# Group sums placed as two 16-bit parts, the mix a slot later, and a new opening and last pass in a graph network layer

## The chip, the cores and the metric

The kernel runs on one core of one Trainium2 chip. The metric is the device time of one execution in microseconds (us); lower is better. A core has five engines with a queue each: TensorE (PE, matmuls), VectorE (DVE), ScalarE (ACT), GpSimd (POOL) and SyncE (SP, which here only issues transfers). Matmuls write to eight PSUM banks of 128 x 512 f32. The engines wait for each other by semaphores that the kernel sets by hand.

## What is computed

x has 6250 rows of 512; 100000 edges (src, dst, weight) are sorted by dst. The rest is weights. Cut to what matters, without the biases' names:

```python
xn  = layernorm(x)
gnn = segment_sum(weight[:, None] * xn[src], dst) @ Wg + b_g
q, k = elu(xn @ Wq + bq) + 1, elu(xn @ Wk + bk) + 1      # 8 heads of 64
v    = xn @ Wv + bv
kv   = einsum('shd,she->hde', k, v)
z    = 1 / einsum('shd,hd->sh', q, k.sum(0))
mix  = einsum('shd,hde,sh->she', q, kv, z) @ Wp + bp
x1   = x + gnn + mix
xm   = layernorm(x1)
g    = mean over rows of (relu(xm @ G1.T + b) @ G2.T + b2)   # 8 gates
W1m, W2m, b1m, b2m = W + sum_e g[e] * tvW[e], ...           # merged weights
res  = xm + relu(xm @ W1m.T + b1m) @ W2m.T + b2m
out  = x1 + layernorm(res) * lng + lnb
```

## The kernel before

The rows are 49 tiles of 128 (T = 49, the last one short). Every f32 factor of a large product is held as two f16 parts (high and low), and a product is three f16 passes over them: 12 matmuls of 128x512 for a tile and a weight of 512 x 512. The accumulator `acc` holds all rows of x in SBUF.

*Opening and head.* SP loads Wg, Wk and Wq into `stage`, the biases, x and the edges; DVE takes the weights' maxima, POOL spreads them over the partitions, DVE makes the scales, ACT the high parts of the weights and DVE the low parts. Then 49 row ticks: layernorm (ACT `normalise`, DVE `low_parts`), stores of the f16 parts of x to `x_rows` and, transposed on PE, to `xt_rows`, and y = xn @ Wg, stored to `y_rows`. The work of each engine for one tick is written in its own `head_tick`.

*The middle.* It runs in slots s. The edges are cut into 196 groups of 512 (NGR), one for each slot; in a slot POOL issues four indirect gathers of 128 rows of `y_rows` each, for a ring of three groups. PE's `part(s)` sums each 128 edges of a group into 32 targets with 12 matmuls against 0/1 times weight matrices (`hots`), which gives a bank of 128 partial rows. `keep_part(s)` on ACT copies the bank to `part32` in f32, `place(s)` on PE moves the rows to their place in a tile with a f32 matmul against a 0/1 matrix (`plc`), and `add_group(s)` on DVE adds the bank to the two tiles of `acc` that it may touch. Around these, tiles of the attention part run at fixed slots: K tile t at slot -2 + 11t/6 (`k_product` on PE; `feature` on ACT and `k_whole` on DVE one slot later; `k_higher`, `k_lower`, `k_sum`; `m_product`, k times x, on PE three slots later, with x reloaded from `x_rows` as two f16 parts). From slot 89 (TURN) the K sums are turned and merged into `KVP`. From slot 95 Q tile t runs at slot 95 + 2t: `q_product`, `feature` one slot later, DVE's `q_shares` (kf, qk, den, rden, qs), `q_higher` and `q_lower` two slots later, `turn_q` on PE at three, `mix` (KVP with the turned q) on PE at four and `add_mix` on DVE at five. The order of work on each engine is that of a loop over the slots, written out for each engine:

```python
for s in range(K_FIRST, SLOTS_END):          # PE
    turn_q(tile at s - 3); part(s); mix(tile at s - 4)
    m_product(tile at s - 3); place(s - 1)
    k_product or q_product(tile at s)
for s in range(K_FIRST, SLOTS_END):          # DVE
    add_group(s - 2); add_mix(tile at s - 5)
    k_sum, k_lower, q_lower(tile at s - 2)
    place_pair or hot_pair; k_whole or q_shares(tile at s - 1)
```

*Tail, gate and last pass.* The tail normalises `acc` and makes the gate's hidden layer. The gate merges the weights; PE waits for all eight `tvW2` blocks and DVE splits b2 in three parts while it does. The last pass runs over the tiles: `hidden` and the second product on PE, residual `res`, bn_stats, bn_aggr, `nbr` and the gain `zr` on DVE, `zr` = res scaled and shifted on ACT, and on POOL two additions, `acc` + lnbb and `ob` = `zr` + `acc`; SP stores `ob`.

## Time and profile before

| | us |
|---|---|
| median of 3 runs | 1880.41 |
| lowest, highest | 1877.25, 1880.98 |
| the profiled execution | 1881.32 |
| its span, first to last instruction | 1879.5 |
| opening; head | 0 to 41.5; to 238 |
| start of the middle; K part | to 262; to 797 |
| turn to Q; Q part | to 845; to 1445 |
| tail; gate | to 1634; to 1676 |
| last pass | to 1879.5 |

A row of a timeline has a start, a duration, the engine, the line of the kernel and the operation, what it writes and reads, how many instructions are merged in it (x12), and in brackets how long the engine stood idle before it and what ended the wait. "issue" is idle time for which the profile shows nothing; "remote" a releaser that it doesn't know. In a table by stretches each engine has its busy time with the number of its instructions; PEclk is the granted clock of PE as a share of the full one.

### The profile page before, as it was taken

The numbers are of one execution on the slowest core, as the hardware profiler recorded it, in microseconds if no ns is written. First come the engines' busy times: TensorE is split into PE (matmuls) and PEld (weight loads), VectorE is DVE, ScalarE is ACT, GpSimd is POOL, SyncE is SP. The second block draws the span as 40 slices with busy tenths as digits, with TensorE's granted clock in tenths as the row PEclk, the third lists the DMA queues.
The fourth block names the chain that finished last, engine by engine and source line by source line (L and its number), as shares of the span: only waits on it lengthen the run. The fifth ranks groups of instructions, "written<-read, shape, count | busy, mean of one in ns | idle before, by whom it ended". The sixth has DMA issues, their size and how long they took to land.

```text
span 1879.5 us, 27602 instructions
## 1 busy us (share of the span) xinstructions
PE 1549.2 (82%) x8551; PEld 672.3 (36%) x8551; DVE 1212.1 (64%) x2230; ACT 702.8 (37%) x1098; POOL 919.1 (49%) x919
## 2 busy tenths in 40 slices
PE   0699968888988898787888888888887799888883
PEld 0345423333333333243333333333333444453331
DVE  7888734554544555456776777676667666468996
ACT  3266522222222232212332333333333677425554
POOL 3000056666666666646666666666663000016776
PEclk9799989999999999978999999999999799989996
DMA  5389777777777777746666666666665422333332
GB/s 182 127 297 324 272 238 227 220 214 224 225 227 223 227 225 225 213 123 193 194 197 200 196 195 196 195 196 197 196 197 154 159 78 79 115 115 107 134 134 83
DMA packets 149271, 353.64 MB, mean 188 GB/s; under 512 B 24773, under 2 KB 30551, under 8 KB 149155
## 3 DMA queue, kind: packets, MB, share of 16 engines
q0 software_dynamic: 62720, 205.57, 37.0%
q1 hardware_dynamic: 84926, 145.42, 22.6%
q8 instruction: 60, 0.98, 0.2%
q10 hardware_dynamic: 1509, 1.21, 0.2%
q14 instruction: 56, 0.46, 0.1%
HBM read 287.93 MB, written 65.38 MB: 188 GB/s over the span
## 4 chain that ended last, share of the span: by engine, by line
PE 37%; DVE 18%; another core or an unknown queue 16%; issue 14%; ACT 9%; DMA 2%; DVEq 1%; ACTq 0%; SPq 0%; POOL 0%; POOLq 0%
PE bank L1550 26%; PE bank L1659 4%; PE bank L1633 4%; ACT mb L642 2%; PE bank L1649 2%; DVE acc L1164 2%; ACT part L636 2%; DVE st L1058 1%; PE bank L1592 1%; ACT qT L663 1%; DVE res L1511 1%; DVE zr L1539 1%; DVE zl L1092 1%; ACT zh L598 1%
## 5 line engine op out<-in xcount | busy, mean ns | idle before, releaser
L850 POOL DMA_INDIRECT rows<-y_rows,idxT x784 | 767.9, 979 | 613.3 <-issue 395.1
L1164 DVE SCALAR_TENSOR_TENSOR acc<-bank,maskt,acc 128x512 f32 x392 | 275.4, 744 | 200.3 <-remote 107.4
L642 ACT ACTIVATE mb<-bank,ones,ncols 128x512 f32<-128x512 f32 x98 | 76.6, 782 | 527.5 <-remote 290.6
L1550 PE MATMUL bank<-KVP,qT 128*128 128x512 f16 x588 | 168.2, 446 | 72.1 <-ACT qT L663 62.1
L1649 PE MATMUL bank<-rows,hots 128*32 128x512 f16 x2352 | 194.3, 402 | 38.7 <-issue 35.1
L1659 PE MATMUL bank<-part,plc 128*128 128x512 f32 x392 | 212.1, 622 | 12.3 <-ACT part L636 6.0
L636 ACT COPY part<-bank 128x512 f32<-128x512 f32 x196 | 113.0, 577 | 192.7 <-remote 145.5
L1550 PE MATMUL bank<-Wg,xtb 128*128 128x512 f16 x588 | 143.3, 396 | 25.6 <-DVE xtb L1103 25.5
L1550 PE MATMUL bank<-Wk,xta 128*128 128x512 f16 x588 | 142.9, 394 | 1.2 <-issue 1.0
L1633 PE MATMUL bank<-xr,kh 128*128 128x512 f16 x392 | 124.8, 402 | 16.7 <-DVE kl L1191 13.4
L1649 PEld LDWEIGHTS bank<-rows,hots 128*32 128x32 f16 x2352 | 78.1, 143 | 166.4 <-issue 144.3
L1550 PE MATMUL bank<-Wq,xta 128*128 128x512 f16 x588 | 135.4, 380 | 0.0
L1550 PE MATMUL bank<-ztg,G 128*128 128x512 f16 (+1 forms) x624 | 134.8, 368 | 0.0
L1550 PEld LDWEIGHTS bank<-KVP,qT 128*128 128x128 f16 x588 | 61.0, 111 | 174.5 <-ACT qT L663 81.4
L1205 DVE SCALAR_TENSOR_TENSOR kf<-bank,cols,mb 128x512 f32<-128x512 f32 x49 | 36.8, 750 | 111.8 <-ACT mb L645 86.6
L1184 DVE SCALAR_TENSOR_TENSOR kf<-bank,cols,mb 128x512 f32<-128x512 f32 x49 | 36.6, 746 | 106.9 <-issue 55.7
L874 POOL PARTITION_ALL_REDUCE mxa<-mx x1 | 0.3, 350 | 206.5 <-DVE mx L1462 206.5
L1659 PEld LDWEIGHTS bank<-part,plc 128*128 128x128 f32 x392 | 68.2, 193 | 67.3 <-issue 45.1
L891 POOL TENSOR_TENSOR ob<-zr,acc 128x512 f32<-128x512 f32 x49 | 63.0, 1287 | 55.4 <-DVE zr L1539 53.3
L1550 PEld LDWEIGHTS bank<-Wg,xtb 128*128 128x128 f16 x588 | 56.7, 101 | 92.8 <-DVE xtb L1103 19.7
L1550 PEld LDWEIGHTS bank<-Wk,xta 128*128 128x128 f16 x588 | 55.1, 100 | 76.4 <-issue 22.6
L1550 PE MATMUL bank<-xd,W1m 128*128 128x512 f16 (+1 forms) x312 | 72.6, 387 | 9.9 <-DMA xd<-zt_rows 6.2
(278 smaller groups left out, 2324.0 us busy)
## 6 DMA issues: line engine op xcount, KB each, us to landing
xta<-xt_rows SPq DMA_DIRECT2D x98, 256.0 KB
x_rows<-xhl SPq DMA_DIRECT2D x49, 256.0 KB, 2.6
xt_rows<-xtb SPq DMA_DIRECT2D x49, 256.0 KB, 3.0
y_rows<-yb SPq DMA_DIRECT2D x49, 256.0 KB, 2.5
rows<-y_rows,idxT POOLq DMA_INDIRECT x784
xr<-x_rows SPq DMA_DIRECT2D x49, 256.0 KB
zt_rows<-ztg SPq DMA_DIRECT2D x49, 256.0 KB, 2.0
acc<-in_x SPq DMA_DIRECT2D x48, 256.0 KB, 3.1
```

What stands on the lines that cost most here:

```text
L598: nc.scalar.activation(to, flat(acc, t), ACT.Identity, scale=rs[:, bass.ds(t, 1)], bias=nb[:, bass.ds(t, 1)]).then_inc(loop.high, 1)
L636: nc.scalar.copy(part32[:, s % 2, :], edge_bank(s)[:, :]).then_inc(part_kept, 1)
L642: nc.scalar.activation(mb[:, :], of[:, :], ACT.Relu, scale=ncols[:, col:col + 1], bias=ones[:, 0:1]).then_inc(f_min, 1)
L850: pool.indirect_dma_start(out=rows[:, slot].rearrange("p a d -> p (a d)"), out_offset=None, in_=y_rows, in_offset=bass.IndirectOffsetOnAxi ...
L891: pool.tensor_tensor(ob[:, b, :], zr[:, b, :], flat(acc, t), ALU.add).then_inc(ob_made, 1)
L1164: nc.vector.scalar_tensor_tensor(out=flat(acc, tile + m), in0=placed_bank(s)[:, :], scalar=maskt[:, m, s:s + 1], in1=flat(acc, tile + m), ...
L1184: nc.vector.scalar_tensor_tensor(out=kf[:, b, :], in0=bank[5][:, :], scalar=cols[:, 1:2], in1=mb[:, :], op0=ALU.mult, op1=ALU.max).then_in ...
L1205: nc.vector.scalar_tensor_tensor(out=kf[:, 0, :], in0=q_bank(t)[:, :], scalar=cols[:, 2:3], in1=mb[:, :], op0=ALU.mult, op1=ALU.max).then_ ...
L1550: ins = nc.tensor.matmul(dest, lhs, rhs, start=(n == 0 and only), stop=(n == len(pairs) - 1), skip_group_check=not only)
L1633: ins = nc.tensor.matmul(bank[c][:, :], (kh, kl)[p][:, b, s], xr[:, b, q, :], start=isinstance(t, int) and t == 0 and i == 0, stop=isinsta ...
L1649: ins = nc.tensor.matmul(edge_bank(s)[W * i:W * i + W, :], hots[:, k, p, :, m + i], rows[:, K4 * (s % RING) + i, q, :], start=n == 0, stop ...
L1659: nc.tensor.matmul(placed_bank(s)[:, :], plc[:, s // WG % 3, s % WG, :], part32[:, s % 2, :], start=True, stop=True).then_inc(placed, 1)
```

## The change

Place: `keep_part` becomes `part_higher`, which writes the bank times 2^-14 as f16; a new `part_lower` on DVE makes the rest, bank times 2^-14 less the high part, from the same bank; `place` is two f16 matmuls that add up. `plc` is f16 and written in another layout. The factors of the weights and of the mask are changed to fit. `mix` and `add_mix` run one slot later.

Opening: only Wg is loaded first, on ACT's queue; the x tiles come ahead of the edges, the biases last. Wk and Wq are loaded at tick 40 of the head (KQ_AT), the edges are packed in memory at tick 41, their maxima are taken at ticks 42 and 43, the scales at 44, the high parts at 45 and 46, the low parts at 47 and 48. Both bias splits and their copies are POOL's, after the scales. x isn't stored as parts; in the K part raw x is loaded again, ACT's `x_again` makes both x and its f16 part, and DVE's `x_lower` the rest. Wp is loaded after the K part, gfc1 at Q tile 3, and the maximum and the scale of gfc1 are taken at slots TURN + 18 and TURN + 28.

Gate and last pass: `tvW2` comes in pairs and PE adds pair by pair; the split of b2 stands after the merged W1. In the last pass the mean comes from the sum that `res` yields beside its output, the variance from a Square on ACT with a sum; DVE makes `cen` and `ob`, POOL keeps only `acc` + lnbb, and the result is stored five tiles later instead of four.

```diff
@@ constants
-SLOTS_END = max(NGR + 2, Q_FIRST + Q_SPACE * (T - 1) + 6)
+SLOTS_END = max(NGR + 2, Q_FIRST + Q_SPACE * (T - 1) + 7)
+PART, WEIGHT = float(2.0 ** -14), float(2.0 ** -8)
+OUT_LAG = 5
+TV2_PAIRS = ((6, 7), (0, 1), (2, 3), (4, 5))
+KQ_AT = (T // U - 1) * U
@@ SP, head_stores
-                if exists(g, j):
-                    t = tile_at(g, j)
-                    sp.wait_ge(head.low, t + 1)
-                    sp.dma_start(row_tile(x_rows, t), xhl[:, j % 4].rearrange("p a d -> p (a d)")
-                                 ).then_inc(x_kept[j % 4], 16)
+                if isinstance(g, int) and tile_at(g, j) == KQ_AT:
+                    sp.wait_ge(tabled, 3)
+                    for k, (dest, w) in enumerate(((Wkraw, Wk), (Wqraw, Wq))):
+                        sp.dma_start(dest[:, :, :], w.rearrange("(c p) n -> p c n", p=P)).then_inc(w_loaded[k + 1], 16)
+                if isinstance(g, int) and tile_at(g, j) == KQ_AT + 1:
+                    pack_edges()
@@ SP, load_rows
-                at_least(sp, m_done, t - 1)
-                sp.dma_start(xr[:, b].rearrange("p a d -> p (a d)"), row_tile(x_rows, t)).then_inc(xr_in[b], 16)
+                at_least(sp, xr_high, 2 * (t - 1))
+                    sp.dma_start(xraw[:, b], row_tile(x[0:(T - 1) * P, :], t)).then_inc(xr_in[b], 16)
@@ ACT
-                nc.scalar.copy(part32[:, s % 2, :], edge_bank(s)[:, :]).then_inc(part_kept, 1)
+                nc.scalar.activation(phl[:, s % 2, 0, :], edge_bank(s)[:, :], ACT.Copy, scale=PART).then_inc(part_high, 1)
+            def x_again(t):
+                b = t % 2
+                act.wait_ge(xr_in[b], 16 * (t // 2) + 16)
+                at_least(act, xr_low, t - 1)
+                at_least(act, m_done, t - 1)
+                for to in (xn32[:, b, :], xr[:, b, 0, :]):
+                    nc.scalar.activation(to, xraw[:, b, :], ACT.Identity, scale=rs[:, t:t + 1], bias=nb[:, t:t + 1]
+                                         ).then_inc(xr_high, 1)
@@ DVE, the middle
+            def part_lower(s):
+                dve.wait_ge(part_high, s + 1)
+                at_least(dve, placed, s - 1)
+                nc.vector.scalar_tensor_tensor(out=phl[:, s % 2, 1, :], in0=edge_bank(s)[:, :], scalar=PART,
+                                               in1=phl[:, s % 2, 0, :], op0=ALU.mult, op1=ALU.subtract).then_inc(part_low, 1)
+            def x_lower(t):
+                b = t % 2
+                dve.wait_ge(xr_high, 2 * t + 2)
+                at_least(dve, m_done, t - 1)
+                nc.vector.tensor_tensor(xr[:, b, 1, :], xn32[:, b, :], xr[:, b, 0, :], ALU.subtract).then_inc(xr_low, 1)
                 add_group(s - 2, tile)
+                part_lower(s - 1)
+                if s == TURN + 18:
+                    gate_largest()
+                if s == TURN + 28:
+                    gate_scale()
-                t = tile_of(q_slot, s - 5)
+                t = tile_of(q_slot, s - 6)
@@ PE, the middle
-                pe.wait_ge(part_kept, s + 1)
+                pe.wait_ge(part_low, s + 1)
-                nc.tensor.matmul(placed_bank(s)[:, :], plc[:, s // WG % 3, s % WG, :], part32[:, s % 2, :],
-                                 start=True, stop=True).then_inc(placed, 1)
+                accumulate(placed_bank(s)[:, :], [(plc[:, s // WG % 3, :, s % WG], phl[:, s % 2, h, :]) for h in range(2)]
+                           ).then_inc(placed, 1)
-                t = tile_of(q_slot, s - 4)
+                t = tile_of(q_slot, s - 5)
@@ ACT, the last pass
+                    nc.scalar.activation(squares[:, :], res[:, j1, :], ACT.Square, bias=negm[:, par, i:i + 1],
+                                         accum_out=dev2[:, par, i:i + 1]).then_inc(squared, 1)
-                    nc.scalar.activation(zr[:, b, :], res[:, j4, :], ACT.Identity, scale=rsr[:, j4 // Q4, j4 % Q4:j4 % Q4 + 1],
-                                         bias=nbr[:, j4 // Q4, j4 % Q4:j4 % Q4 + 1]).then_inc(zr_made, 1)
@@ POOL, the last pass
-                    pool.tensor_tensor(ob[:, b, :], zr[:, b, :], flat(acc, t), ALU.add).then_inc(ob_made, 1)
@@ DVE, the last pass
-                    nc.vector.bn_stats(st6[:, j % Q4, :], res[:, j, :]).then_inc(six_made, 1)
-                    nc.vector.tensor_tensor(zr[:, b, :], zr[:, b, :], lngb[:, :], ALU.mult).then_inc(gained, 1)
+                    nc.vector.scalar_tensor_tensor(out=cen[:, :], in0=res[:, j5, :], scalar=negm[:, par5, i5:i5 + 1],
+                                                   in1=lngb[:, :], op0=ALU.add, op1=ALU.mult).then_inc(gained, 1)
+                    nc.vector.scalar_tensor_tensor(out=ob[:, b5, :], in0=cen[:, :], scalar=rsr[:, par5, i5:i5 + 1],
+                                                   in1=flat(acc, t5), op0=ALU.mult, op1=ALU.add).then_inc(ob_made, 1)
```

Three places show how instructions move. First PE in the Q part, one tile (two slots), from the turning of a q on: `hots` with `rows` is a part, `plc` a place, `KVP` the mix, `Wq` the next product. Before:

```order
L1691 MATMUL bank<-ident_51,qhl 128x128 x8
L1649 MATMUL bank<-rows,hots 32x512 x12
L1659 MATMUL bank<-part_146,plc 128x512
L1649 MATMUL bank<-rows,hots 32x512 x12
L1550 MATMUL bank<-KVP_113,qT 128x512 x12
L1659 MATMUL bank<-part_146,plc 128x512
L1550 MATMUL bank<-qrows,ones_54 128x512
L1550 MATMUL bank<-Wq_104,xta 128x512 x12
```

After:

```order
L1772 MATMUL bank<-ident_51,qhl 128x128 x8
L1730 MATMUL bank<-rows,hots 32x512 x12
L1631 MATMUL bank<-KVP_116,qT 128x512 x12
L1631 MATMUL bank<-phl,plc 128x512 x2
L1730 MATMUL bank<-rows,hots 32x512 x12
L1631 MATMUL bank<-phl,plc 128x512 x2
L1631 MATMUL bank<-qrows,ones_54 128x512
L1631 MATMUL bank<-Wq_107,xta 128x512 x12
```

The mix has moved from between the second part and its place to between the first part and its place, and each place is two matmuls.

Second DVE in the Q part, from the last step of the shares to the end of the same slot. `acc<-bank,maskt,acc` twice is `add_group`, `phl` the new low part, `acc<-bank,cols,acc` is `add_mix`. Before:

```order
L1225 TENSOR_TENSOR qs<-qk,rden 128x512
L1295 TENSOR_LOAD tileof
L1295 ISA x2
L1164 ISA
L1164 SCALAR_TENSOR_TENSOR acc<-bank,maskt,acc 128x512
L1164 ISA
L1164 SCALAR_TENSOR_TENSOR acc<-bank,maskt,acc 128x512
L1232 SCALAR_TENSOR_TENSOR qhl<-qs,qhl 128x512
L1138 TENSOR_TENSOR plc<-iota_100,tgt 128x128x2
```

After:

```order
L1297 TENSOR_TENSOR qs<-qk,rden 128x512
L1377 TENSOR_LOAD tileof
L1377 ISA x2
L1221 ISA
L1221 SCALAR_TENSOR_TENSOR acc<-bank,maskt,acc 128x512
L1221 ISA
L1221 SCALAR_TENSOR_TENSOR acc<-bank,maskt,acc 128x512
L1231 SCALAR_TENSOR_TENSOR phl<-bank,phl 128x512
L1240 SCALAR_TENSOR_TENSOR acc<-bank,cols,acc 128x512
L1304 SCALAR_TENSOR_TENSOR qhl<-qs,qhl 128x512
L1195 TENSOR_TENSOR plc<-iota_103,tgt 128x256
```

The low part stands behind the shares and the group's adds; `add_mix` has come from the other slot of the tile.

Third DVE in the last pass, one tile. Before:

```order
L1511 SCALAR_TENSOR_TENSOR res<-bank,cols,zq 128x512
L1516 BN_STATS st_59<-res 128x6
L1520 RECIPROCAL rsr<-sd_60 128x4
L1522 SCALAR_TENSOR_TENSOR nbr<-var_58,rsr 128x4
L1539 TENSOR_TENSOR zr<-zr,lngb 128x512
```

After:

```order
L1594 SCALAR_TENSOR_TENSOR res,rsum<-bank,cols,zq 128x512
L1605 SCALAR_TENSOR_TENSOR cen<-res,negm,lngb 128x512
L1609 TENSOR_SCALAR negm<-rsum 128x1
L1612 REGISTER_ALU
L1617 ISA
L1617 SCALAR_TENSOR_TENSOR ob<-cen,rsr,acc 128x512
```

Statistics and gain are gone, `cen` and `ob` stand behind the residual of a later tile.

## Rows read from the trace of the kernel before

**Rows 1.** The page: the span, and its groups of instructions for mix and Wq product.
```profile
span 1879.5 us, 27602 instructions
...
L1550 PE MATMUL bank<-KVP,qT 128*128 128x512 f16 x588 | 168.2, 446 | 72.1 <-ACT qT L663 62.1
...
L1550 PE MATMUL bank<-Wq,xta 128*128 128x512 f16 x588 | 135.4, 380 | 0.0
```

**Rows 2.** Table by stretches: length, busy us of each engine, clock, DMA share, GB/s.
```profile
41.50:238.00 196.50, 165.95 (x1009) 85.54 (x1009) 157.91 (x316) 104.57 (x157) 0.86 (x2) 0.93 0.70 249
262.00:797.00 535.00, 468.00 (x2475) 180.91 (x2473) 275.38 (x501) 149.36 (x235) 346.37 (x359) 0.96 0.73 222
845.00:1445.00 600.00, 518.29 (x2994) 217.64 (x2994) 416.12 (x741) 192.97 (x296) 388.51 (x392) 0.94 0.67 195
1676.00:1879.50 203.50, 154.69 (x631) 58.31 (x631) 165.35 (x248) 110.31 (x161) 132.13 (x98) 0.89 0.32 113
```

**Rows 3.** Timeline of one tile, Q part: start, duration, engine, line, [idle before <-releaser].
```profile
952.10 0.95 POOL L850 DMA_INDIRECT rows<-y_rows,idxT  x1 [0.30 <-issue]
...
953.01 2.76 PE L1550 MATMUL bank<-Wq,xta 128*128 128x512 f16 x12
...
955.81 0.78 ACT L642 ACTIVATE mb<-bank,ones,ncols 128x512 f32<-128x512 f32 x1 [5.72 <-issue]
...
957.29 0.75 DVE L1205 SCALAR_TENSOR_TENSOR kf<-bank,cols,mb 128x512 f32<-128x512 f32 x1 [1.12 <-issue]
...
958.01 0.88 PE L1649 MATMUL bank<-rows,hots 128*32 128x512 f16 x12
...
959.81 1.46 POOL L850 DMA_INDIRECT rows<-y_rows,idxT  x1 [1.78 <-PE bank L1649]
...
960.66 1.41 DVE L1164 SCALAR_TENSOR_TENSOR acc<-bank,maskt,acc 128x512 f32 x2 [0.21 <-issue]
...
961.13 4.37 PE L1550 MATMUL bank<-KVP,qT 128*128 128x512 f16 x12 [2.25 <-ACT qT L663]
...
965.30 1.14 PE L1659 MATMUL bank<-part,plc 128*128 128x512 f32 x2
...
966.69 2.76 PE L1550 MATMUL bank<-Wq,xta 128*128 128x512 f16 x12
```

**Rows 4.** Timeline, Q part, a mix after a shorter wait.
```profile
1216.27 2.76 PE L1550 MATMUL bank<-KVP,qT 128*128 128x512 f16 x12 [0.51 <-ACT qT L663]
```

**Rows 5.** Timeline of the K part at 499 us.
```profile
499.93 2.76 PE L1550 MATMUL bank<-Wk,xta 128*128 128x512 f16 x12
...
503.43 0.60 PE L1633 MATMUL bank<-xr,kh 128*128 128x512 f16 x2
...
503.87 0.38 PE L1633 MATMUL bank<-xr,kl 128*128 128x512 f16 x1
...
506.87 0.78 ACT L642 ACTIVATE mb<-bank,ones,ncols 128x512 f32<-128x512 f32 x1 [5.98 <-remote]
```

**Rows 6.** Timeline of the opening and of the start of K.
```profile
14.65 10.65 SPq L432 DMA_DIRECT2D srow<-in_dst  x1
...
41.51 0.80 PE L1592 MATMUL bank<-ident,xhl 128*128 128x128 f16 x6 [41.51 <-DVE xhl L1092]
...
248.28 0.58 PE L1550 MATMUL bank<-krows,ones 3*128 3x512 bf16 x1 [11.76 <-DMA xta<-xt_rows]
```

**Rows 7.** Groups with shapes kept apart: the weights' maxima, the gain in the last pass.
```profile
L1539 DVE TENSOR_TENSOR zr<-zr,lngb 128x512 f32<-128x512 f32 x49 | 63.2, 1289 | 15.1 <-ACT zr L774 14.6
...
L938 DVE TENSOR_REDUCE mx<-stage 128x1 f32<-128x2048 f32 x3 | 6.9, 2285 | 7.5 <-DMA stage<-in_L_gnn_weight 3.4 <-DMA stage<-in_L_mix_Wk 2.2 <-DMA stage<-in_L_mix_Wq 2.0
```

**Rows 8.** Timeline of the last pass: its first and last residual, a gain behind it.
```profile
1682.05 0.75 DVE L1511 SCALAR_TENSOR_TENSOR res<-bank,cols,zq 128x512 f32<-128x512 f32 x1 [3.90 <-PE bank L1550]
...
1858.87 0.74 DVE L1511 SCALAR_TENSOR_TENSOR res<-bank,cols,zq 128x512 f32<-128x512 f32 x1
...
1867.19 0.69 DVE L1539 TENSOR_TENSOR zr<-zr,lngb 128x512 f32<-128x512 f32 x1 [0.40 <-ACT zr L774]
```

371 lines of the change are left out of this document (210 added, 161 removed).

## The prediction

> **What bounds the kernel now.** I read the head of the page, then the table by stretches, then short timelines inside the two long stretches, since those show which wait ends last. The profiled execution's span is 1879.5 us [rows 1] and its own time 1881.32, so 1.8 us lie around the span; the median of the three runs, 1880.41, is 0.9 below that execution. The stretches [rows 2] are the opening to 41.5, the head (49 row tiles) to 238, the K part of the middle 262 to 797, the Q part 845 to 1445 and the last pass from 1676. K and Q hold 1135 of the 1880 us. In K 89 groups of edges pass in 535 us, 6.0 us each; in Q 49 tiles pass at two groups each, 12.1 us a tile. PE is the busiest engine in both (468.0 of 535, 518.3 of 600), but it isn't full, and POOL needs less than the time that passes too: a gather is issued every 0.95 + 0.30 = 1.25 us [rows 3], a group has four of them, so POOL could start a group every 5.0 us, 10.0 a Q tile.
>
> The loop that ends last in Q reads off one tile [rows 3]: the product of x and Wq starts at 953.01; ACT's feature starts 2.80 later, when the product ends; DVE's first step at 957.29; its last step of the shares is over before the adds of the even group at 960.66 (1.41 us). Beside it PE waited 2.25 us for the turned q and then ran the mix in 4.37 us. Another mix, after a wait of 0.51 us, took 2.76 [rows 4]. Over all 49 tiles such idle is 62.1 us, 1.3 a tile, and a matmul of the mix takes 446 ns in the mean where one of the Wq product takes 380 [rows 1]: 12 × 0.066 = 0.8 us a tile, so about half of the mixes run slow. The place at 965.30 and the next product at 966.69 stand behind the mix. 1.3 + 0.8 is the 2 us a tile between POOL's 10.0 and 12.1.
>
> In K one fact limits what a timeline proves: the product is recorded from 499.93 for 2.76 us, yet the feature starts at 506.87 and the trace names no releaser [rows 5]. There PE's recorded ends are early, or something outside the records holds. I keep wide bounds for it.
>
> **The change, part by part.**
>
> *Place in two 16-bit matmuls.* Before, a place is two f32 passes; from the place at 965.30 to the next product with its bias rows between are 1.39 us [rows 3], some 0.95 of them the place. Two f16 matmuls of the same 128x512 occupy 503.87 − 503.43 = 0.44 us [rows 5]. PE saves 0.51 us a group, 1.0 in two groups. ACT's copy from the bank becomes a scaled one (a tenth of a us more, ACT is idle two thirds of the time) and is free. DVE gains an operation per group, with the bank and one other operand, 0.75 us as kf at 957.29 [rows 3], and has a shorter comparison for places, which now writes 16 bits; that is under +1.5 on some 8.5 us of DVE work a Q tile, beside 12.1 us: DVE isn't the bound by its sum.
>
> But it is on the path now. The low part of group s−1 stands behind the adds of group s−2, and in the Q part these stand behind the feature and the shares. The loop becomes: product 2.80, feature to the first DVE step 1.48, shares to the start of the adds 3.37, adds 1.41, low part 0.75, then place and bias rows 1.39 less 0.51, and the next product: **10.7 us a tile**, by rows of the clear case [rows 3]. From the product's end to the place are 7.0 us. PE has for them: turning q, a part and a place (2.2 us to 958.01, now 0.5 less), a part of 0.88 and a mix at full clock of 2.7, in all 5.3. It will stand 1.7 us before that place.
>
> *Mix one slot later.* The turned q is then ready a slot ahead, and the 2.25 us wait at 961.13 goes [rows 3]. What is late next is just this place: the idle moves from before the mix to before the place. The question is PE's clock. The mix took 4.37 after 2.25 us of idle and 2.76 after 0.51 [rows 3, 4]; 1.7 lies nearer the first. If the product behind the place then runs at the lower level of 1.2 GHz, the loop is 10.7 + 1.6 = 12.3. The Trainium skill ("TensorE: Matmul & The Clock Gate", section "HAM oscillation — how this bites in real kernels") says that a kernel whose PE keeps pausing falls to the lower clock again and again; by that the Q part would stay at 12.3 a tile. The mix at 4.37 agrees, the mix at 2.76 shows that a short pause does nothing. I take the middle, 11.5, since about half of the mixes now run slow after a wait: 49 × −0.6 = **−29 us** (ends: −69 and +10).
>
> *K part.* The same place saving, 0.51 of PE a group; added are two ACT passes over 512 columns that remake x (0.78 each, as the feature's at 955.81 [rows 3]) and one DVE subtraction (0.7, under kf's 0.75) a K tile, against a reload of the same 256 KB. ACT is busy 149 of 535 us, DVE 275 [rows 2], so they hide; if the subtraction came to stand ahead of the low part, a tile would lose up to its 0.7. The lower bound is POOL's 10.0 for two groups where 12.0 pass: 44.5 × −2.0 = −88; the upper is 0, since the place also gets its new wait there and the DMA engines are already busy 0.73 of the time [rows 2]; at 10.0 they would be at 0.88, above the 0.70 and 0.73 of the busiest stretches there. I take half: **−44**.
>
> *Opening.* Only Wg is loaded ahead of the first tile. The first transposes start at 41.51 [rows 6]. Two maxima of 2.29 us [rows 7], their waits for weights, half of the scale chain, the low part of Wk (2048 columns like a maximum, about 2.3) and the split of a bias on DVE leave the stretch before it. Two ways bound it: SP stays blocked for 10.65 us on the small row of edges at 14.65 [rows 6], which no longer stands ahead of the first four x loads but still ahead of the next (−16), or it doesn't block (−26). I take **−19**. What is moved comes back in ticks 42 to 48 of the head, where DVE is busy 158 of 196.5 us and PE 166 [rows 2]: 2 × 2.3 for maxima, 2 × 2.3 for low parts and 14 small operations of 0.2 = 12.0, plus 0.9 for the edge scales, **+13**; SP issues the two loads and seven small ones in ticks 40 and 41, ahead of that tick's stores: **+3** (0 to +8). The stores of x_rows go, 12.8 MB where the DMA engines are busy 0.70 of the time [rows 2]: **−3** (−6 to 0). At the start of K the first product waited 11.76 us for its data [rows 6] behind weights of which one load is now elsewhere: **−3** (−6 to 0). POOL now splits both biases after tick 44; it ends just before K starts, by the old split's pace, 0 to +4. Head together **−9** (−22 to +4).
>
> *Gate.* Loads by pairs let PE work as data comes; the b2 split leaves slack and stands on DVE's path with five operations of at most 0.69 each, 3.4 us. Net **+1.5** (−2 to +4). The gate maximum (2.29) leaves the start of the tail: **−1**. It now stands in the Q part, once.
>
> *Last pass.* 48 tiles from 1682.05 to the last residual at 1858.87 [rows 8], 3.68 us each. On DVE a tile had residual, statistics, gain 1.29 mean, hidden's low part; POOL two adds. Now DVE has residual 0.74, centring 0.75, a small negation 0.15, result 0.75, hidden's part 0.4: 2.8, with two operations of two SBUF inputs beside one POOL add. The gain is 0.69 when alone and 1.29 in the mean [rows 7, 8], so 0.6 is lost to POOL a tile; with one POOL add left I keep 0.6: 3.4. That is 48 × −0.28 = **−13**. The Trainium skill ("SBUF — State Buffer", section "Who interferes with whom") calls the port pair of DVE and GpSimd an exclusive lock; the rows at 0.69 against a mean of 1289 ns agree. If both new operations paid 0.6, a tile would take 4.0 and the pass would lose 15 instead. The end, 20.6 us from that residual to the span's end, holds a ping-pong of ACT, DVE and POOL for five tiles; without POOL's add in each: **−4**. Together −17 (−30 to +11).
>
> **The sum:** −9 − 44 − 29 − 1 + 1.5 − 17 = −98.5. 1881.3 − 98.5 = 1782.8; less 0.9 to the median: **1782**.
>
> **The rivals.**
> A. *The forecast*, about 1782; own range 1735 to 1820. For it: PE's idle before the mix goes by the order alone, and the place is half as long. 0.50.
> B. *The middle keeps its pace.* 6.0 and 12.1 stay, because gathers and their landing (or what the trace doesn't name at 506.87) set them. For it: unnamed releasers, DMA at 0.73 and 0.67. Against: POOL's own pause before a group is ended by a part on PE, 1.78 us at 959.81 [rows 3]. Only the ends gain, −9 − 1 + 1.5 − 17 = −25.5: 1855. 0.25.
> C. *The floors are reached*: 10.0 in K, 10.7 in Q, full clock. −25.5 − 88 − 69: 1698. Against: nothing in the trace runs long at POOL's own pace. 0.12.
> D. *Slower.* The place waits behind DVE's chain and PE's clock falls each time: place, bias rows and product at the lower level put 1.6 + 0.9 us on the loop, 13.2 a Q tile (49 × 1.1 = +54), and in K 0.2 for two groups (+9); with the ends −25.5 that is +37.5: 1918. It decides from the point at which the pause before the place costs as much clock as the mix's did and reaches the place itself. For it: 4.37 against 2.76. Against: PE's pause would be shorter than the mix's. 0.09.
> E. *It doesn't do what it says:* the wait for the turned q stays, or the loads in ticks 40 to 48 disturb the head by more than the opening gains; all terms cancel, 1880. 0.04.
>
> **How the numbers follow.** The likeliest is A, 1782. The range reaches to B's 1855 with a few us for the last pass's bound, and down to 1700, which leaves out most of C and D: 1700 to 1860. A run of this kernel can be told from no change at about 0.2% (3.8 us). Faster: A, B, C and half of what is left of E, 0.89; slower 0.09; same 0.02.
>
> **What would show it.** In Q: period between Wq products, 11.5 (B 12.1, C 10.7, D 13.2); PE's largest wait is that of the place for phl from DVE, 1.5 to 2 us, and none for qT is left; products of 4.4 us after it mean the lower clock. In K: 11.0 for two groups, POOL's waits shorter. Opening: first transposes at about 22. Head: ticks 42 to 48 stretched by some 13 us. Last pass: residuals 3.4 apart, cen or ob near 1.4 in the mean of one of them. I am wrong if the period in Q doesn't change though the mix waits no more, or if the DVE operation isn't what the place waits for.

## The result and the profile after

The changed kernel took 1926.67 us in the median of four runs (1920.8 to 1933.14), the kernel before 1880.0 beside it: a ratio of 1.0251, 95% interval 1.0216 to 1.0287. It is 47 us slower. Forecast was 98 faster, in a range of 1700 to 1860. What came is near the rival called slower (D, 1918). Its mechanism is there in part: the place waits behind VectorE's chain, and PE's clock falls behind it in some tiles. That the sum is so near is luck, as the table below shows: D had +54 in Q, +9 in K and −25.5 at the ends, and +14.5, +25.5 and about 0 came, with 2.6 more in the turn and 9.3 behind the last product. The profiled execution has a span of 1931.3 us, 51.8 more than before [rows 1]; it is the longest of the four, 6.5 us over their median.

The page after, the groups that answer to [rows 1] and the place:

```profile
span 1931.3 us, 28100 instructions
...
L1631 PE MATMUL bank<-phl,plc 128*128 128x512 f16 x392 | 129.2, 414 | 224.5 <-DVE phl L1231 161.0
...
L1631 PE MATMUL bank<-Wq,xta 128*128 128x512 f16 x588 | 180.0, 470 | 0.0
...
L1631 PE MATMUL bank<-KVP,qT 128*128 128x512 f16 x588 | 137.6, 383 | 3.4 <-issue 3.4
```

A matmul of the Wq product takes 470 ns where it took 380, one of the mix 383 where it took 446, and PE stands idle for 224.5 us before places, 161 of them ended by VectorE's low part `phl`. The table by stretches, as in [rows 2]:

```profile
41.50:238.00 196.50, 156.60 (x949) 79.97 (x947) 152.28 (x303) 98.80 (x146) 20.88 (x24) 0.92 0.58 193
262.00:797.00 535.00, 422.83 (x2365) 159.46 (x2364) 336.42 (x620) 204.08 (x317) 342.78 (x345) 0.91 0.70 214
845.00:1445.00 600.00, 470.79 (x2869) 190.11 (x2868) 441.95 (x822) 187.94 (x283) 376.26 (x382) 0.89 0.64 189
1676.00:1931.00 255.00, 195.22 (x894) 88.43 (x891) 177.61 (x349) 119.63 (x228) 73.13 (x51) 0.87 0.33 113
```

The granted clock falls from 0.96 to 0.91 in K and from 0.94 to 0.89 in Q; no engine is busier than 0.79 of Q. One tile of the Q part, the engines of [rows 3]:

```profile
960.88 0.68 DVE L1231 SCALAR_TENSOR_TENSOR phl<-bank,phl 128x512 f16<-128x512 f32 x1
...
961.61 0.61 PE L1631 MATMUL bank<-phl,plc 128*128 128x512 f16 x2 [2.89 <-DVE phl L1231]
...
962.15 0.39 PE L1631 MATMUL bank<-qrows,ones 3*128 3x512 bf16 x1
...
962.47 4.45 PE L1631 MATMUL bank<-Wq,xta 128*128 128x512 f16 x12
...
966.96 0.78 ACT L669 ACTIVATE mb<-bank,ones,ncols 128x512 f32<-128x512 f32 x1 [6.47 <-PE bank L1631]
```

PE waits 2.89 us for the low part, the place follows, and the product behind it takes 4.45 us instead of 2.76. In K and Q 36 of 98 such products take 4 us or more; before it was 4.

Where the 51.8 us are, by the times at which work of the same kind starts (first transposes, first part, last Wk product, first and last Wq product, last mix, first copy of a turned tile in the tail, last gate activation, first and last residual of the last pass, end of span):

| stretch | before | after | difference | forecast |
|---|---|---|---|---|
| opening | 41.5 | 21.2 | −20.3 | −19 |
| head to first part | 221.1 | 235.1 | +14.1 | +10 |
| K part | 511.8 | 537.3 | +25.5 | −44 |
| turn | 65.2 | 67.8 | +2.6 | 0 |
| Q part | 587.8 | 602.3 | +14.5 | −29 |
| last product to last mix | 13.7 | 23.0 | +9.3 | 0 |
| tail | 193.7 | 195.4 | +1.6 | −1 |
| gate to first residual | 47.2 | 51.5 | +4.2 | +1.5 |
| last pass | 176.8 | 180.9 | +4.0 | −13 |
| end | 20.6 | 17.0 | −3.7 | −4 |

### The profile page after: what moved, and what is told of

The parts are those of the page before. It is cut to its first block and busy times, and to the rows that moved or that the text cites. A ratio compares the mean times of both kernels' runs of the same rounds, so it can differ in the third digit from the quotient of the medians.

```text
span 1931.3 us, 28100 instructions
## 1 busy us (share of the span) xinstructions
PE 1506.3 (78%) x8551; PEld 645.9 (33%) x8551; DVE 1305.7 (68%) x2516; ACT 771.6 (40%) x1244; POOL 877.6 (45%) x884
## 3 DMA queue, kind: packets, MB, share of 16 engines
q1 hardware_dynamic: 78623, 132.68, 20.5%
## 5 line engine op out<-in xcount | busy, mean ns | idle before, releaser
L1631 PE MATMUL bank<-phl,plc 128*128 128x512 f16 x392 | 129.2, 414 | 224.5 <-DVE phl L1231 161.0
L1631 PE MATMUL bank<-Wq,xta 128*128 128x512 f16 x588 | 180.0, 470 | 0.0
L663 ACT ACTIVATE phl<-bank 128x512 f16<-128x512 f32 x196 | 114.8, 586 | 156.9 <-remote 86.9
L1730 PE MATMUL bank<-rows,hots 128*32 128x512 f16 x2352 | 176.0, 405 | 0.3 <-issue 0.3
L1631 PE MATMUL bank<-Wk,xta 128*128 128x512 f16 x588 | 164.1, 438 | 0.0
L1631 PE MATMUL bank<-KVP,qT 128*128 128x512 f16 x588 | 137.6, 383 | 3.4 <-issue 3.4
L1231 DVE SCALAR_TENSOR_TENSOR phl<-bank,phl 128x512 f16<-128x512 f32 x196 | 133.0, 679 | 0.0
L1631 PEld LDWEIGHTS bank<-phl,plc 128*128 128x128 f16 x392 | 31.2, 101 | 295.8 <-DVE phl L1231 189.5
L932 POOL TENSOR_TENSOR acc<-acc,lnbb 128x512 f32 (+1 forms) x49 | 72.4, 1478 | 117.7 <-ACT zq L794 117.7
L1631 PEld LDWEIGHTS bank<-Wq,xta 128*128 128x128 f16 x588 | 63.9, 116 | 102.5 <-issue 68.2
```

The source lines that it names most:

```text
L663: nc.scalar.activation(phl[:, s % 2, 0, :], edge_bank(s)[:, :], ACT.Copy, scale=PART).then_inc(part_high, 1)
L932: pool.tensor_tensor(flat(acc, t), flat(acc, t), lnbb[:, :], ALU.add).then_inc(based, 1)
L1231: nc.vector.scalar_tensor_tensor(out=phl[:, s % 2, 1, :], in0=edge_bank(s)[:, :], scalar=PART, in1=phl[:, s % 2, 0, :], op0=ALU.mult, op1= ...
L1631: ins = nc.tensor.matmul(dest, lhs, rhs, start=(n == 0 and only), stop=(n == len(pairs) - 1), skip_group_check=not only)
L1730: ins = nc.tensor.matmul(edge_bank(s)[W * i:W * i + W, :], hots[:, k, p, :, m + i], rows[:, K4 * (s % RING) + i, q, :], start=n == 0, stop ...
```

## Experiments

The kernels ran on four chips: beside e1 to e4 the kernel before took 1882 us, beside e6 to e9, on another, 1868, beside all others, on two more, 1728 to 1730. I call the last two clean. Nearly all of the difference lies in the middle: on the clean chip K takes 443.7 us instead of 511.8, the turn 51.0 instead of 65.2 and Q 509.7 instead of 587.8, while opening, head, last pass and end agree to 2 us, tail and gate together to 3, and from the last product to the last mix it takes 4 longer. So ratios are to the kernel before on the same chip, run beside it.

Each stretch below is read from one profiled execution, and these differ by some us where nothing was changed: e2 alters nothing in K, and its K is 507.2 beside 511.8. Single differences under about 5 us in a stretch prove nothing. The edits are shown shortened to their point.

### One part alone, one part undone (chip of 1882)

e1, place alone in the kernel before:

```diff
-    nc.scalar.copy(part32[:, s % 2, :], edge_bank(s)[:, :])
+    nc.scalar.activation(phl[:, s % 2, 0, :], edge_bank(s)[:, :], ACT.Copy, scale=PART)
     add_group(s - 2, tile)
+    part_lower(s - 1)
-    matmul(placed_bank(s), plc, part32)
+    accumulate(placed_bank(s), [(plc, phl high), (plc, phl low)])
```

> The kernel before with one part of the change alone: the place in two 16-bit matmuls, its low part made by VectorE behind the adds; the mix stays at slot + 4 and opening and last pass stay. Theory 1 (the place now waits for VectorE's low part, which stands behind the feature, the shares and the adds, and PE's clock falls behind that wait): the K part gets slower by some 20 us and the Q part by 10 to 40, since both the mix and the place now end a wait there: 1910 to 1940. Theory 2 (the middle lost time by the x that is made again in the K part and by the work that was moved into it, not by the place): the place saves PE 0.5 us a group, so 1840 to 1880.

Measured: 1884.66, ratio 1.0015 (0.998 to 1.0049). K 517.3 (+5.5), Q 581.0 (−6.8). Neither theory: no gain of 0.5 us a group, and no loss beyond the noise as long as the mix stands where it stood.

e2, mix alone:

```diff
-                t = tile_of(q_slot, s - 4)
+                t = tile_of(q_slot, s - 5)
                 if t is not None:
                     mix(t)
```

> The kernel before with the mix and its addition one slot later, nothing else. Theory 1 (PE's idle before the mix and its slow mixes cost 2 us a Q tile): the wait for the turned q goes, the Q part falls from 588 us to 540 to 570, and the end of the middle grows by one slot: 1840 to 1875. Rival (gathers or another loop set 12 us a Q tile, and the idle only moves): the Q part stays within 5 us of 588 and the total is 1880 to 1890.

Measured: 1866.95, ratio 0.9927 (0.9899 to 0.9955). The wait for the turned q is gone (3.5 us of idle in place of 72.1 [rows 1]) and a mix matmul takes 389 ns instead of 446, 2 us a tile:

```profile
L1550 PE MATMUL bank<-KVP,qT 128*128 128x512 f16 x588 | 141.4, 389 | 3.5 <-issue 3.3
```

But Q (572.7) gains only 15.1 us, 0.3 a tile, and the end of the middle gives 6.8 back. The total lies in the range of theory 1, but not the Q part, which was to fall to 540 to 570. The 2 us were not what stood between GpSimd's 10.0 and the 12.1.

e3, the changed kernel with the place of before:

```diff
-                part_lower(s - 1)
-                accumulate(placed_bank(s), [(plc, phl high), (plc, phl low)])
+                matmul(placed_bank(s), plc, phl in f32)
```

> The changed kernel with the place of before: f32 copy by ScalarE, f32 matmul, no low part on VectorE; all the rest as changed. Theory 1 (place): from first part to last K product 510 to 518 us instead of 538, Q part under 588, total 1850 to 1880. Theory 2 (the x made again costs the K part its 26 us): that stretch stays at 535 to 540, total 1900 to 1925.

Measured: 1891.85, ratio 1.0046 (1.0021 to 1.0071) where the changed kernel had 1.0251, so some 38 us less. K 519.7, Q 578.4. The total lies between the two theories. Beside the rest of the change the place costs 18 of K's 25.5 us and 24 in Q; 8 us of K are left, little over the noise, of which x made again is the likeliest cause. Alone the place cost 5.5 in K and nothing in Q (e1). So in K place and x made again cost more together than apart, and in Q the place costs only beside something else, most likely the mix's new slot; neither pair was run by itself.

e4, the low part earlier, and in the last pass the hidden layer's low part earlier:

```diff
                 add_group(s - 2, tile)
-                part_lower(s - 1)
...
+                part_lower(s)
                 for slot_of, after, work in ((k_slot, 1, k_whole), (q_slot, 1, q_shares)):
@@ last pass, DVE
                 res of tile t
+                hidden_low(...)
                 cen, negm, ob
-                hidden_low(...)
```

> The changed kernel with two orders on VectorE changed. The low part of group s is made at the end of slot s, ahead of the feature's and the shares' work, instead of behind the adds of slot s + 1. In the last pass the low part of the hidden layer stands right behind the residual, ahead of centring and result. Theory 1 (what costs is where the low part stands): PE's wait for it all but goes, the K part falls under 512 us and the Q part to 540 to 575. Theory 2: both keep 538 and 602. In the last pass, if the lock between VectorE's operations and GpSimd's addition hit the hidden layer's low part (1598 ns in place of 804) and this operation holds PE, a tile falls from 3.77 to 3.3 to 3.5 us, 13 to 20 us in all; if PE or ScalarE sets the pace, it stays at 3.7. Total by theory 1: 1810 to 1860; by theory 2 with the lock gone: 1905 to 1915.

Measured: 1885.83, ratio 1.0022 (0.9995 to 1.0049) where the changed kernel had 1.0251: some 43 us of the 47 are back, 20.5 of them by the last pass (160.4 instead of 180.9, 3.34 us a tile) and 23 in Q (579.1). The idle before places that VectorE's low part ends falls from 161 us to 11. But K stays at 532.0, and Q and the total are above what theory 1 had for them: for the middle it came only in part.

The last pass is settled by two views. The changed kernel, three groups of VectorE and a tile:

```profile
L1582 DVE SCALAR_TENSOR_TENSOR hT<-h,sc,hT 128x512 f16<-128x512 f32 x24 | 38.4, 1598 | 2.3 <-ACT hT L786 2.3
L1605 DVE SCALAR_TENSOR_TENSOR cen<-res,negm,lngb 128x512 f32<-128x512 f32 x49 | 38.2, 780 | 0.1
L1617 DVE SCALAR_TENSOR_TENSOR ob<-cen,rsr,acc 128x512 f32<-128x512 f32 x49 | 36.8, 751 | 9.5 <-DVE cen L1605 8.0
...
1803.02 1.44 POOL L932 TENSOR_TENSOR acc<-acc,lnbb 128x512 f32 x1 [2.54 <-ACT zq L794]
1803.26 1.75 DVE L1582 SCALAR_TENSOR_TENSOR hT<-h,sc,hT 128x512 f16<-128x512 f32 x1
...
1805.14 0.38 PE L1631 MATMUL bank<-krows,qrows 3*128 3x512 bf16 x1 [2.56 <-DVE hT L1582]
```

The same groups in e4:

```profile
L1620 DVE SCALAR_TENSOR_TENSOR ob<-cen,rsr,acc 128x512 f32<-128x512 f32 x49 | 55.3, 1128 | 9.5 <-DVE cen L1608 8.0
...
L1608 DVE SCALAR_TENSOR_TENSOR cen<-res,negm,lngb 128x512 f32<-128x512 f32 x49 | 39.6, 808 | 0.1
...
L1582 DVE SCALAR_TENSOR_TENSOR hT<-h,sc,hT 128x512 f16<-128x512 f32 x24 | 23.9, 995 | 2.3 <-ACT hT L786 2.3
```

GpSimd's addition starts after 2.54 us of idle, when the residual has let ScalarE make the next input; then VectorE is at the hidden layer's low part, which takes 1.75 instead of 0.75, and PE waits 2.56 us for it. In e4 the same overlap falls on `ob` (1128 instead of 751), for which no engine waits.

### The clean chip (1728)

> The kernel before, unchanged, so that its trace and that of the changed kernel come from one chip. The time of the kernel before was 1882 us beside e1 to e4 and 1728 beside e5 and p1 to p3; the middle alone makes the difference. If the chip is one where gathers land fast, Q takes 10.2 to 10.6 us a tile and PE's or GpSimd's waits name the gathers or nothing; if it is one where they land slowly, 12.0.

> The changed kernel, unchanged. Theory 1 (the place behind VectorE's low part is a loop of its own, 12.3 to 12.6 us a Q tile whatever the gathers do): on a chip where the kernel before takes 1728, the changed one takes 1830 to 1900, a larger loss than the 2.5% on the first. Theory 2 (a chip's gathers set the pace of both kernels and the change adds a fixed piece to it): 1.02 to 1.03 on every chip, 1763 to 1780 there.

Measured: the kernel before 1728.6, the changed kernel 1774.65 (1762.94 to 1775.14), ratio 1.0265 (1.024 to 1.0291); K 443.7 to 456.0, Q 509.7 to 531.3. By its number that is theory 2, the same loss on every chip; the loop of theory 1 with its 12.3 to 12.6 us a tile didn't come. Here each feature on ScalarE starts 0.04 us behind the recorded end of its product, in all Q tiles of both kernels, so that PE's rows can be read. GpSimd in the kernel before, and PE's waits in its Q part:

```profile
1010.03 0.95 POOL L850 DMA_INDIRECT rows<-y_rows,idxT  x1 [0.30 <-issue]
...
1011.28 1.30 POOL L850 DMA_INDIRECT rows<-y_rows,idxT  x1 [0.30 <-issue]
...
1012.89 1.38 POOL L850 DMA_INDIRECT rows<-y_rows,idxT  x1 [0.30 <-issue]
...
1014.57 0.95 POOL L850 DMA_INDIRECT rows<-y_rows,idxT  x1 [0.30 <-issue]
...
POOL rows L850 <- issue: 100.5, 330, 0.3
...
PE bank L1649 <- DMA rows<-y_rows,idxT: 29.7, 26, 2.3
```

GpSimd never stops: 0.30 between gathers, some of 1.3 in place of 0.95, 1.02 in the mean, and PE waits 26 times for rows. Eight times 1.02 + 0.30 are 10.6 us, and Q takes 10.62 a tile: the kernel before runs it at GpSimd's own pace. The changed kernel, two tiles, a stretch of each in the table, and its waits:

```profile
1023.68 0.61 PE L1631 MATMUL bank<-phl,plc 128*128 128x512 f16 x2 [1.77 <-DVE phl L1231]
...
1024.53 2.77 PE L1631 MATMUL bank<-Wq,xta 128*128 128x512 f16 x12
...
1034.24 0.61 PE L1631 MATMUL bank<-phl,plc 128*128 128x512 f16 x2 [1.76 <-DVE phl L1231]
...
1035.10 2.76 PE L1631 MATMUL bank<-Wq,xta 128*128 128x512 f16 x12
...
935.35 0.61 PE L1631 MATMUL bank<-phl,plc 128*128 128x512 f16 x2 [1.76 <-DVE phl L1231]
...
936.21 4.45 PE L1631 MATMUL bank<-Wq,xta 128*128 128x512 f16 x12
...
937.00:940.00 3.00, 3.00 (x9) 1.07 (x7) 2.46 (x6) 0.00 (x0) 2.39 (x3) 0.51 0.75 209
1025.00:1027.00 2.00, 2.00 (x11) 0.94 (x10) 2.00 (x5) 0.00 (x0) 1.67 (x2) 1.00 0.81 231
...
PE bank L1631 <- DVE phl L1231: 66.3, 39, 2.1
```

The loop of the forecast is there to a tenth or two: products start 10.57 us apart (34 of 48 periods within 10.50 to 10.62; forecast 10.7), and 12.24 to 12.61 where the product behind the place ran at the lower level, 0.51 of the clock (9 of 48, 7 of them under 12.3; forecast 12.3). Three more slow products stand at the start, with periods of 12.4 to 14.4. The wait for the low part is 1.76 us in both tiles shown, so the wait alone doesn't decide the clock; twelve of 49 products were slow. The mean is 11.07 beside 10.62. At full clock the new loop is as long as GpSimd's eight gathers, and PE waits for rows only 3 times here; what Q loses, 21.6 us, lies in the tiles with a slow product.

p1, three gathers a group instead of four, in the kernel before (a quarter of the rows is left out):

```diff
-                for k in range(K4):
+                for k in range(K4 if s < RING else 3):
...
-                pe.wait_ge(gathered[s % RING], 16 * K4 * (s // RING + 1))
+                pe.wait_ge(gathered[s % RING], 16 * (K4 + 3 * (s // RING)))
```

> A probe on the kernel before: from the fourth group on GpSimd gathers three of the four blocks of rows of a group, the fourth block is left as it was, so the output is wrong. GpSimd's and the DMA engines' work for a group falls by a quarter. Rival B (gathers and their landing set the 12.0 us a Q tile): the Q part falls from 588 us to 480 to 540 and the K part likewise. Theory 1 (the loop over PE, ScalarE and VectorE sets it): Q within 575 to 590 us, K 500 to 515.

> The probe with three gathers of four (a quarter of the rows is left out, so the output is wrong), to see it beside the kernels of this call. If gathers set the pace of the middle on this chip, K and Q come down to PE's own 9.7 us a Q tile; where the loop over the engines sets it, Q stays at its 12.0.

Measured: 1655.1 and 1653.28, both on clean chips, one each: 0.9578 and 0.9565. K 420.9 in both, Q 467.8 and 463.5. Two tiles and a stretch of the Q part, with PE's busy time behind its length:

```profile
1179.07 2.76 PE L1550 MATMUL bank<-Wq,xta 128*128 128x512 f16 x12
...
1188.75 2.76 PE L1550 MATMUL bank<-Wq,xta 128*128 128x512 f16 x12
...
760.00:1190.00 430.00, 430.00 (x2702) 186.20 (x2700) 369.66 (x667) 172.69 (x266) 280.56 (x267) 1.00 0.67 193
```

With three gathers of four all Q tiles but the first two take 9.68 us, and PE is busy all the time: that is PE's own work. So on this chip four gathers cost the kernel before 0.9 us a tile over PE, and only that is there to be won.

p2, one of the three passes of the mix:

```diff
-                                               for p, q in PASSES]).then_inc(mix_done, 1)
+                                               for p, q in PASSES[:1]]).then_inc(mix_done, 1)
```

> A probe on the kernel before: the mix is made of the high parts alone, 4 matmuls in place of 12, so part of the output is less exact. PE has 1.8 us less a Q tile. If PE's work or the loop through the mix sets the pace, the Q part falls by 49 x 1.8 = 88 us or, where the next thing is late soon, by 30 at least; if gathers set it, by under 10. K stays.

Measured: 1712.17, 0.9908 (0.9888 to 0.9928). Q 494.8: 15 us for 90 us less of PE's work. That is between the two conditions (under 10, 30 at least), but much nearer the first: PE's work isn't the bound, though it still counts a little.

p3, one add a group instead of two:

```diff
-                for m in range(2):
-                    nc.vector.scalar_tensor_tensor(out=flat(acc, tile + m), in0=placed_bank(s)[:, :],
...
+                nc.vector.scalar_tensor_tensor(out=flat(acc, tile), in0=placed_bank(s)[:, :],
+                                               scalar=maskt[:, 0, s:s + 1], in1=flat(acc, tile),
+                                               op0=ALU.mult, op1=ALU.add).then_inc(edge_added, 2)
```

> A probe on the kernel before: each group's sums are added to the first of their two tiles only, so the output is wrong. VectorE has 0.7 us less a group, and what stands behind the adds comes 0.7 earlier. If a loop that goes through VectorE's adds sets the pace, Q falls by 49 x 0.7 to 49 x 1.4, 34 to 69 us, and K by some 30; if gathers or PE set it, both by under 10.

Measured: 1736.46, 1.0053 (1.0034 to 1.0072): Q 520.0, ten more with 0.7 us less on VectorE in each slot. The adds aren't the bound; why it got slower I didn't find out.

e5, e4 with one more edit, x made again behind the high part on ScalarE:

> The kernel of e4 with one more order changed: in the K part ScalarE makes x again after its copy of the group's sums (the high part) instead of ahead of it. Theory 1 (in K the two passes of 0.8 us stand ahead of the high part and with it ahead of the place): the K stretch falls from 532 us to 505 to 520, the rest stays, 1858 to 1875. Rival (something else gives the middle its pace of about 6 us a group): the K stretch stays at 528 to 536 and the total at 1886.

```diff
-  ((k_slot, 1, k_feature), (k_slot, 1, x_again), (q_slot, 1, q_feature), ...
+  ((k_slot, 1, k_feature), (q_slot, 1, q_feature), ...
                 part_higher(s)
+                x_again(tile at s - 1)
```

Measured: 1705.04 beside 1728.25, 0.9865 (0.9849 to 0.9882), and as e10 once more 0.9855 (0.9821 to 0.9889). The expectation had times for a chip of 1882, so it can't be held against this one. K is 445.5 where the changed kernel has 456.0, Q 502.7 where it has 531.3. PE's idle before places falls from 143.5 us to 2.7, and now the gathers end its waits:

```profile
L1634 PE MATMUL bank<-phl,plc 128*128 128x512 f16 x392 | 120.1, 389 | 2.7 <-DVE phl L1234 2.7
...
POOL rows L904 <- issue: 100.1, 329, 0.3
...
PE bank L1733 <- DMA rows<-y_rows,idxT: 58.3, 60, 6.9
```

c1, the kernel before with the mix one slot later and the new last pass in the order of e4 (place, opening and head as before):

```diff
-                t = tile_of(q_slot, s - 4)
+                t = tile_of(q_slot, s - 5)
@@ last pass, DVE
                 res of tile t
+                hidden_low(...)
+                cen, negm, ob
-                statistics and gain
```

> The kernel before with two parts of the change: the mix one slot later, and the new last pass with the low part of the hidden layer ahead of centring and result. Place, opening, x_rows and gate as before. If the parts add up, it is 15 us faster by the mix and 20 by the last pass (16 in it, 4 at its end): a ratio of 0.980 to 0.984 on a chip of 1880, and 0.984 to 0.990 where gathers set the middle and the mix gains nothing.

Measured: 1706.8, 0.9857 (0.9814 to 0.9901), and as c2 once more 0.9844. The last pass alone is 16 and its end 3.5 us shorter; the mix gains nothing where gathers set the pace (Q 509.5 beside 509.7), as expected.

> The kernel of e5 again, beside c1's. On a chip where the kernel before takes 1730, 0.986 as before. On one of 1870 to 1880 it should be e6's 1.000 less the 13 us that e7 and e9 had less than e6 in K: 0.992 to 0.995.

> The kernel of c1 again, beside e5's: f32 place, mix one slot later, new last pass with the hidden layer's low part first. On a chip of 1730, 0.986 as before; on one of 1870 to 1880 the mix's 15 us come on top of the pass's 20: 0.980 to 0.985, and then it is the fastest of all here.

Both ran on a chip of 1730, so the second half of these expectations wasn't tried.

### What is left (chip of 1868)

e6 is the kernel of e4 once more, on this chip. e7, e8 and e9 all have e5's place for x; beyond that, against e5:

```diff
@@ e7, DVE
+                part_lower(s - 1)
                 add_group(s - 2, tile)
...
-                part_lower(s)
@@ e8, ACT, DVE and PE
-                nc.scalar.activation(phl[:, s % 2, 0, :], edge_bank(s)[:, :], ACT.Copy, scale=PART)
+                nc.scalar.copy(phl[:, s % 2, :], edge_bank(s)[:, :])
...
-                part_lower(s)
...
-                accumulate(placed_bank(s), [(plc, phl high), (plc, phl low)])
+                matmul(placed_bank(s), plc, phl in f32)
@@ e9, PE
-                t = tile_of(q_slot, s - 5)
+                t = tile_of(q_slot, s - 4)
```

> The kernel of e4 again, beside others of one call: low part early, hidden layer's low part early, x made again ahead of the high part in K. e5 differs from it in the last point alone. If the order of x and high part costs K something, its K stretch is 5 to 20 us longer than that of e5 (445 on a chip of 1728, some 15 less than e4's 532 on a chip of 1880); if not, the two agree within 3.

> As e5, but the low part of group s - 1 stands at the start of slot s, right ahead of the adds of group s - 2, instead of at the end of slot s - 1. It is then still behind the feature and the shares, 1.4 us earlier than in the changed kernel. Theory 1: PE's pause before the place shrinks by 1.4 of 2 to 3 us, so the Q part comes most of the way to e5's: a third of the loss is left. If the whole chain ahead counts, no gain.

> As e5, but the place is that of before: f32, no low part. It tells whether the two 16-bit matmuls gain anything once their low part isn't waited for. PE's work for a Q tile is 1.0 us more. If gathers set the pace of the middle, it is within 10 us of e5; if PE does, 40 us slower.

> As e5, but the mix and its addition one slot earlier, as before the change. With the wait for the low part gone, the wait for the turned q comes back: the Q part 0 to 15 us longer than e5's on a chip where gathers are slow, as in e2, and the end of the middle 5 us shorter; within 5 us of e5 where gathers set the pace.

| kernel | ratio, interval | K | Q |
|---|---|---|---|
| e6, x ahead of the high part | 1.0001 (0.9977 to 1.0025) | 519.0 | 571.9 |
| e7, low part ahead of the adds | 0.9946 (0.9918 to 0.9973) | 504.2 | 576.7 |
| e8, f32 place | 0.9890 (0.9862 to 0.9917) | 511.4 | 572.2 |
| e9, mix at its old slot | 0.9966 (0.9939 to 0.9993) | 506.0 | 581.1 |

The kernel of e5 itself wasn't run on this chip, so each of e7, e8 and e9 differs from e6 in two things, and their expectations against e5 can't be held against a run.

In the K part, where no mix is, e9 differs from e6 only by the place of x on ScalarE. Its K is 13 us shorter, but the turn behind it is 11 longer (73.7 beside 62.6), so the profiled executions alone don't show what the two passes ahead of the high part cost. The medians are 1870.1 for e6, 1862.2 for e9 and 1858.3 for e7; by them x ahead of the high part costs some 8 to 12 us in all, if what else differs costs nothing. e7, with the low part of the group before ahead of the adds, has 15 less in K and 4.8 more in Q than e6: taken from behind the adds it is nearly as good as a slot's end, though 18 of its 49 Wq products take 4 us or more where 2 of e6's do. In e9 the wait for the turned q is back (69.4 us): its Q is 9 longer than e6's, and the end of the middle gives 8.7 back. e8: beside e7, which it equals but for the place and its low part, the f32 place is 12 us faster, beside e9, which also has the mix elsewhere, 16. Its granted clock is 0.936 in the profiled execution, that of e6, e7 and e9 0.905 to 0.909. PE works 1 us a tile more with it, and more at the higher level. That this is why e8 is faster is argued, not shown.

## Why the prediction was wrong

*What bounds the kernel.* This is the step that failed. It read the 1.3 us of idle and 0.8 us of slow mix a tile as the distance from GpSimd's 10.0 to the 12.1 that pass. They only filled it. e2 took both away and Q gained 0.3 us a tile; e4 took nearly all of the waits for the low part away and Q stayed at 12.06; p2 took 1.8 us of PE's work away on the clean chip and won 0.3. Something else sets 12.0 on the first chip. On the clean one 10.6 is set by the gathers (p1: 9.68 with three of four). That was rival B, which named both: the gathers, and what the trace doesn't name at 506.87. The floor of 10.0 was also too low: with the mean gather in place of one of 0.95 us, eight are 10.4 us on the first chip and 10.6 on the clean one. The rows spoke for B where the prediction noted unnamed releasers and went on.

*The new loop.* Right in size: forecast 10.7 and 12.3, measured 10.57 and 12.26 on the clean chip. Wrong was what it was compared with. It doesn't take the place of a slower loop: the bound was elsewhere, so a wait taken away before the mix wins little, while the new one before the place costs wherever PE's clock falls behind it. Q rose from 12.25 to 12.55 us a tile on the first chip and from 10.62 to 11.07 on the clean one.

*PE's pause before the place.* Forecast 1.7, measured 1.76 in most tiles of the clean chip; on the first 1.76 is the commonest too, but others run to 4.8. Whether the product then runs slow was put at one half; it was 12 of 49 and 22 of 49. That a short pause is harmless and a long one not (0.51 and 2.25 [rows 3, 4]) doesn't hold as a rule for pauses between: 1.76 gave both, on the first chip 6 slow products and 14 fast ones.

*K part, −44.* Sign wrong: +25.5. 18 of them go with the place (e3), though alone it cost 5.5 (e1); x made again ahead of the high part costs some 8 to 12 us by e6 against e7 and e9, not cleanly separated. Both lengthen the same chain ahead of the place. The prediction said "they hide", because ScalarE is idle most of the time, and didn't ask what is queued behind them there: the high part, for which VectorE and then PE wait.

*The 16-bit place.* 0.5 us of PE a group was right (the place takes 0.61 us where it took 1.14 [rows 3]), and worth nothing: PE wasn't the bound, and on the chip of 1868 e8 is 12 us faster without it than e7 with it.

*Mix one slot later.* −15.1 in Q alone on the first chip; its end costs 6.8 in e2 and 9.3 in the whole change, not forecast: the last mix and add are one slot later.

*Opening, head, gate, end.* Opening −20.3 for −19, head to first part +14.1 for +10, end −3.7 for −4: these came near enough. The gate's +4.2 for +1.5 is just outside its own (−2 to +4).

*Last pass, −13.* It came to +4.0 because of where the 0.6 us that GpSimd's addition adds fell. It was looked for on `cen` or `ob`, which no engine waits for, and came on the hidden layer's low part, which PE waits for: 804 ns before, 1598 after, 3.77 us a tile in place of 3.4. With the order of e4 it is 3.34, so the sum without that wait was right. That VectorE's operations with two SBUF inputs and GpSimd's exclude each other (the Trainium skill, "SBUF — State Buffer", "Who interferes with whom") agrees with 1.75 beside 0.75 us; which operation pays follows from the order alone.

*The clock.* The Trainium skill's rule in "TensorE: Matmul & The Clock Gate" ("HAM oscillation — how this bites in real kernels"), by which Q would stay at 12.3, says that a PE that keeps pausing falls to the lower clock again and again. It was nearer than the middle that I took: 12.55 on the first chip, though on the clean one only 12 of 49 products ran slow.

**What stays open.** On the chips of 1868 and 1882 other waits than on the clean ones set the middle. In long stretches of the Q part of the kernel before, e2 and e4 the feature starts every 11.9 to 12.4 us whatever the engines' work, for example in e4:

```profile
1202.97 12.30 SPq L506 DMA_DIRECT2D xta<-xt_rows  x2
1202.98 0.78 ACT L669 ACTIVATE mb<-bank,ones,ncols 128x512 f32<-128x512 f32 x1 [5.17 <-remote]
1203.43 0.95 POOL L901 DMA_INDIRECT rows<-y_rows,idxT  x1 [2.20 <-remote]
...
1206.79 2.76 PE L1631 MATMUL bank<-Wq,xta 128*128 128x512 f16 x12
...
1214.95 0.78 ACT L669 ACTIVATE mb<-bank,ones,ncols 128x512 f32<-128x512 f32 x1 [5.11 <-remote]
...
1203.50:1204.00 0.50, 0.50 (x4) 0.24 (x3) 0.00 (x0) 0.47 (x2) 0.50 (x1) 1.00 0.10 25
...
POOL rows L901 <- remote: 82.5, 41, 2.2
...
PE bank L1730 <- DMA rows<-y_rows,idxT: 1.0, 2, 0.8
```

ScalarE, SP and GpSimd are released within half a microsecond, 5.4 us after the recorded end of the product at 1206.79, at 1214.95. The semaphore updates in the trace say more. The product, the turning of q and the part behind it have their recorded ends at 1198.37, 1200.43 and 1201.24; their three signals arrive at 1202.95, 1203.05 and 1203.17. In 27 Q tiles of e4 and 26 of the kernel before the three come within 0.4 us of each other, nearly always 0.09 and 0.22 us behind the first, though the recorded ends lie 1.25 us apart or more; on the clean chip they never do so in the kernel before. So on these chips PE's signals come late and together. In the kernel before the feature starts more than 0.2 us behind its product in 41 of 49 K tiles and 38 of 49 Q tiles, 2.6 and 1.7 us in the mean of all tiles; all ten traces in which the middle is slow, those of the first result too, show such tiles in number, while on the clean chips none does, but for one tile each in e5 and e10, 0.4 us late.

That the gathers' pace sets the 12.0 there, as p1 shows for the clean chip, doesn't fit: in e4's Q part GpSimd itself stops 41 times for some 2 us, and PE waits for rows 1.0 us in all. The dip of the DMA engines at 1203.5 comes behind such a stop of GpSimd. What holds the signals back, and why only in the stretches with gathers, no run shows; p1 wasn't run on such a chip. The chips of 1868 and 1882 were each met in one set of experiments only, so whether it's the chip or its state at the time isn't shown either.

## What to carry to other kernels

A wait that the profile ranks high isn't yet the bound: take it away alone first (here one line) and see if the period moves; a probe that drops a part of one engine's or queue's work can tell in one run what sets the pace, as p1 did. Where an engine starts long after the recorded end of what it waits for, look at when the signal came before reading a loop off the rows. An operation that is cheap by its engine's busy share costs by what is queued behind it there, so put a new producer as early in its engine's order as its input allows, and put the operation that a lock will hit where nobody waits for it. The best of the kernels here, 0.984 to 0.987 of the kernel before on a clean chip (c1, e5) and 0.989 on that of 1868 (e8), all have the new last pass with that order; c1 and e8 do without the 16-bit place.
